# Shared-expert products added earlier in VectorE's search work, and the seam to the routed experts reordered, in a two-layer gated cross-attention kernel

## The reference

```python
x = x + tanh(g_xattn[0]) * xattn0(ctx_512, layernorm(x))      # graph from top-k similarities of ctx
x = x + tanh(g_ffn[0])   * ffn0(layernorm(x))                 # mixture of experts
x = x + tanh(g_xattn[1]) * xattn1(layernorm(x), ctx, ctx)
x = x + tanh(g_ffn[1])   * ffn1(layernorm(x))                 # block-quantized weights

# xattn0, per sequence: sim is 512 x 512
threshold = top_k(sim, 153)[..., -1]
A = sigmoid(sim) * (sim >= threshold);  A = (A + A.T) / 2
return (1 - gamma) * layernorm_x + gamma * A

# ffn0: 8 experts of 352 columns, 2 per token, and a shared one of 704 columns
y      = sum over the token's two experts of weight * (silu(x @ w1) * (x @ w3)) @ w2
shared = (silu(x @ sw1) * (x @ sw3)) @ sw2
return y + shared
```

## Time and profile before

| what | value |
|---|---|
| median of 3 runs | 1660.83 us (1656.81 to 1661.04) |
| the profiled execution | 1661.27 us |
| its span, first to last instruction | 1659.4 us |
| busy: PE, DVE, ACT, POOL | 1467.9, 1207.6, 745.5, 554.1 us |
| chain that ended last, by engine | PE 62%, DVE 20%, issue 6%, POOL 5%, ACT 3%, DMA 2% |

### The profile page before, as it was taken

How to read it: one execution, slowest core, us unless ns; L and a number is a source line. 1 busy time by engine, 2 the same in 40 slices (tenths; PEclk the granted TensorE clock), 3 DMA queues, 4 the chain that set the end, 5 groups by cost and what they waited for, 6 DMA issues and landing times.

```text
span 1659.4 us, 24186 instructions
## 1 busy us (share of the span) xinstructions
PE 1467.9 (88%) x8146; PEld 709.0 (43%) x8146; DVE 1207.6 (73%) x2087; ACT 745.5 (45%) x1346; POOL 554.1 (33%) x530
## 2 busy tenths in 40 slices
PE   3278888886999998399999999988999999999998
PEld 1144454544555554123333333324444444444444
DVE  6987777665999895899898888856556555655565
ACT  3564545223555555167777777761221222122212
POOL 2523323112776674882001000012233323332332
PEclk8589898997999999589999999999999999999999
DMA  4312222124565553663202012353000000000000
GB/s 156 105 52 66 66 66 66 46 69 146 173 199 176 182 181 129 168 149 60 56 2 48 17 18 40 52 93 61 1 0 25 0 0 0 25 0 0 25 13 13
DMA packets 114811, 113.79 MB, mean 69 GB/s; under 512 B 59416, under 2 KB 87320, under 8 KB 114720
## 3 DMA queue, kind: packets, MB, share of 16 engines
q1 hardware_dynamic: 106448, 89.64, 20.1%
q0 software_dynamic: 5680, 18.62, 4.0%
q10 hardware_dynamic: 2592, 4.39, 0.7%
HBM read 59.26 MB, written 31.20 MB: 55 GB/s over the span
## 4 chain that ended last, share of the span: by engine, by line
PE 62%; DVE 20%; issue 6%; POOL 5%; ACT 3%; DMA 2%; SPq 1%; DVEq 0%; POOLq 0%; ACTq 0%
PE PS L2215 18%; PE PS L2238 10%; PE PS L1039 9%; PE PS L1654 6%; PE PS L1643 6%; PE PS L1631 5%; PE PS L1054 4%; DVE WORK L1800 3%; PE PS L2228 2%; POOL WORK L2056 2%; POOL WORK L2063 1%; DVE WORK L695 1%; DVE WORK L722 1%; ACT BIG L1549 1%; DVE WORK L762 1%
## 5 line engine op out<-in xcount | busy, mean ns | idle before, releaser
L2215 PE MATMUL PS<-BIG 128*128 128x512 f16 x1536 | 339.9, 382 | 3.5 <-issue 2.1
L1800 DVE TENSOR_REDUCE WORK<-PS 128x2 f32<-128x1024 f32 x256 | 302.7, 1218 | 39.9 <-PE PS L1631 38.8
L1549 ACT ACTIVATE BIG<-PS 128x512 f32<-128x512 f32 x512 | 278.7, 596 | 91.3 <-PE PS L1643 86.1
L2215 PEld LDWEIGHTS PS<-BIG 128*128 128x128 f16 x1536 | 151.0, 98 | 183.7 <-issue 6.4
L1631 PE MATMUL PS<-BIG 128*128 128x512 f16 x512 | 189.3, 397 | 14.7 <-DVE WORK L1800 7.3
L1643 PE MATMUL PS<-BIG 128*128 128x512 f16 x512 | 193.3, 384 | 2.9 <-ACT BIG L1549 1.9
L1039 PE MATMUL PS<-BIG,WORK 128*128 (+1 forms) x1128 | 178.0, 315 | 16.1 <-DVE WORK L1074 9.6
L2238 PE MATMUL PS<-BIG 128*128 128x512 f16 x768 | 173.8, 379 | 1.8 <-DVE BIG L2310 1.8
L2141 ACT ACTIVATE WORK<-PS 128x512 f32<-128x512 f32 x64 | 38.1, 597 | 298.8 <-PE PS L2215 298.8
L2290 DVE SCALAR_TENSOR_TENSOR BIG<-PS,WORK 128x512 f32<-128x512 f32 x64 | 44.2, 690 | 138.8 <-ACT WORK L2141 138.7
L1039 PEld LDWEIGHTS PS<-BIG,WORK 128*128 128x128 f16 x1128 | 108.6, 98 | 79.0 <-issue 22.6
(11 more groups left out here) (257 smaller groups left out, 2228.5 us busy)
## 6 DMA issues: line engine op xcount, KB each, us to landing
wdq_scratch<-WORK SPq DMA_DIRECT2D x48, 256.0 KB, 2.2
WORK<-in_L_ffn_w_dram SPq DMA_DIRECT2D x32, 352.0 KB, 3.5
y_scratch<-WORK SPq DMA_DIRECT2D x39, 256.0 KB, 2.0
BIG<-BIG SPq DMA_DIRECT2D x96, 64.0 KB, 2.3
X<-in_x_dram SPq DMA_DIRECT2D x4, 1024.0 KB, 9.1
WORK<-in_L_ffn_w_dram SPq DMA_DIRECT2D x16, 256.0 KB, 2.6
WORK<-in_L_ffn_gate_w_dram SPq DMA_DIRECT2D x16, 256.0 KB, 3.2
WORK<-in_L_ffn_up_w_dram SPq DMA_DIRECT2D x16, 256.0 KB, 3.2
```

The source lines that it names most:

```text
L1549: nc.scalar.activation(PB[:, tp, 2 * h + j, :], src, ACT.Exp, scale=SOFT_SCALE).then_inc(exp_ok, 1)
L1800: v.tensor_reduce(MXU[:, g % 2, c:c + 2], APAIR[h % 2], AX_X, ALU.max, negate=True).then_inc(max_ok, 1)
L2215: ins = nc.tensor.matmul(bank[b], fxT[:, p, a, k * P:(k + 1) * P], w[:, c, l, k, :], start=(i == 0), stop=(i == 3 * KD - 1))
```

## The change

In the first stage `y_in` leaves the start of `half(u)` for the first three cycles and is written into the work between the half tiles: the product of the cycle before's last tile inside `search_step(a, 2)` behind its two counting passes; those of the cycle's tiles behind the third of four `window`s, behind `check_threshold`, and behind the second `norm` at the cycle's end. In the last cycle it stays at the start of `half(u)`, but for i = 0.

At the seam, ScalarE's splits of expert 6's first three chunks move from in front of the silu of the last half tile to behind it, and all of expert 7's splits move into the slots (three chunks in slot 0, two each in slots 1 and 2). VectorE does both `rows_hot` before the splits of chunks 1 and 2, and copies the indices (L1265) before it makes the expert table; chunks 3 to 6 of expert 6 are split behind that. In a slot, `fast_lo` moves in front of `w_first`.

```diff
@@ a_scalar, last cycle
-                if i == 7:
-                    act.wait_ge(SH.hg_mm, 2 * TT - 1)
-                    fast_hi(act, 8, E - 2, range(NBUF))
                 act_sil(act, SH, HOME, h, u, pair_of(f, i))
                 act_thi(act, SH, near((u - 1) // 2), 1 - h, u - 1)
...
-            fast_hi(act, 8, E - 2, (NBUF,))
+            fast_hi(act, 8, E - 2, range(NBUF))
             act_thi(act, SH, HOME, 1, 2 * TT - 1)
-            fast_hi(act, 8, E - 2, range(NBUF + 1, NCH))
-            fast_hi(act, 9, E - 1, range(NBUF))
+            fast_hi(act, 8, E - 2, range(NBUF, NCH))
@@ a_vector
-            def search_step(b, n):
+            def search_step(b, n, t=None):
...
+                if t is not None:
+                    y_in(t)
@@ half(u)
-                if h == 0 and t >= 2:
+                if f == B - 1 and h == 0 and i > 0:
                     y_in(t - 2)
@@ cycles
-                search_step(a, 2)
+                search_step(a, 2, t1 - R - 1 if f else None)
                 window((0,))
                 half(u + 2)
                 window((1,))
                 half(u + 3)
-                window((2, 3))
+                window((2,))
+                y_in(t1 - R)
+                window((3,))
                 half(u + 4)
                 pick_threshold()
                 half(u + 5)
                 check_threshold(a)
+                y_in(t1 - R + 1)
                 adjacency(a)
...
                 norm(t1 + 1)
+                y_in(t1 - R + 2)
                 if c < B:
                     search_start(c)
@@ end of the first stage
-            rows_hot(0)
             low(2 * TT - 1)
-            fast_lo(dve, 8, E - 2, range(1, NBUF))
+            rows_hot(0)
             rows_hot(1)
             v.nop().then_inc(hot_ok, 1)
-            fast_lo(dve, 8, E - 2, (NBUF,))
+            fast_lo(dve, 8, E - 2, range(1, NBUF))
             y_in(TT - 1)
-            fast_lo(dve, 8, E - 2, range(NBUF + 1, NCH - 1))
@@ b_scalar, slot
-                if first:
-                    fast_hi(act, 9, E - 1, LAST_CHUNKS[p])
+                if i < len(LAST_CHUNKS):
+                    fast_hi(act, 9, E - 1, LAST_CHUNKS[i])
...
-        LAST_CHUNKS = (range(NBUF, NCH - 2), range(NCH - 2, NCH))
+        LAST_CHUNKS = ((0, 1, 2), (3, 4), (5, 6))
@@ b_vector
+            dve.wait_ge(map_mm, 1)
+            v.tensor_copy(IDX, bank[2][:, 0:SLOTS]).then_inc(idx_ok, 1)
             v.tensor_copy(POS, POSF).then_inc(pos_ok, 1)
...
-            dve.wait_ge(eid_ok, 1)
-            dve.wait_ge(map_mm, 1)
-            v.tensor_copy(IDX, bank[2][:, 0:SLOTS]).then_inc(idx_ok, 1)
-            fast_lo(dve, 8, E - 2, (NCH - 1,))
-            fast_lo(dve, 9, E - 1, range(NBUF))
+            fast_lo(dve, 8, E - 2, range(NBUF, NCH))
             dve_lo(dve, MO, HOME, 0, 0)
@@ b_vector, slot
                 if not last:
                     dve_lo(dve, MO, HOME, 1 - p, i + 1)
+                if i < len(LAST_CHUNKS):
+                    fast_lo(dve, 9, E - 1, LAST_CHUNKS[i])
                 for n in units(i)[0:1]:
                     w_first(dve, link, n)
...
-                if first:
-                    fast_lo(dve, 9, E - 1, LAST_CHUNKS[p])
```

More of the change, by code:

```diff
@@ L926, in a_vector @@
                 dve.wait_ge(xn_st[p], 8 * TT)
+            low(2 * TT - 1)
             rows_hot(0)
-            low(2 * TT - 1)
-            fast_lo(dve, 8, E - 2, range(1, NBUF))
             rows_hot(1)
             v.nop().then_inc(hot_ok, 1)
-            fast_lo(dve, 8, E - 2, (NBUF,))
+            fast_lo(dve, 8, E - 2, range(1, NBUF))
             y_in(TT - 1)
-            fast_lo(dve, 8, E - 2, range(NBUF + 1, NCH - 1))
         class Rows:
```

## The result

The changed kernel takes 1644.03 us (median of 4 runs, 1643.27 to 1649.63) against 1660.93 for the kernel before: a ratio of 0.9909, 95% interval 0.9886 to 0.9933. That is faster, inside the predicted range of 1632 to 1652, and 4 us short of the predicted gain. The profiled execution took 1643.61 us (span 1641.7); busy are PE 1463.1, DVE 1208.8, ACT 745.2 and POOL 555.6 us, all within 5 us of before.

A forecast was written before the change was run, and what follows sets the result against it. It took TensorE and VectorE, neither full, to wait for each other in turn, with TensorE losing 24.9 us to `y_in`. Cycles 17.4, seam 7.1 and slots -3.3 sum to 21.2 off 1661.27: 1640 us, range 1632 to 1652.

The forecast's parts named there:

- The third rival: Cycles: several waits of 0.5 to 3 us could keep the granted clock at 0.50; 24 us slower, 1685; chance 0.04.
- Cycles 2 and 3: VectorE's idle time goes and the fourth window moves behind `y_in`: 6.9 and 6.6 us gained.
- VectorE does set the pace up to step 4: Cycles: the gain follows VectorE's lost idle time and moved windows, not the sum of TensorE's waits of 1.95 and 4.35.
- 3.8 + 0.7: Cycle 1: 3.76 us for the window moved behind `y_in`, plus half of 1.4 us saved on slow matmuls.
- the first rival: Cycles: hidden half tiles become what TensorE waits for, only moved windows count; cycles 10, total 1651 us; chance 0.20.
- The seam: From the last half tile to the routed stage: indices copied 7.1 us earlier, bounds 4 and 8.
- The second condition: Seam: expert 6's last chunk, read only after chunk 3's split, is ready at 378.7 us, against 379.3.
- the fixed distance from transpose to matmuls: Seam: fetch and TensorE's transpose follow the earlier index copy at their distance, so 7.1 us counts as gained.
- So I count no loss: Seam: VectorE's `rows_hot` takes 2.29 us beside GpSimd's multiplication and 2.28 without, so running them together costs nothing.
- The slots: Slot 2: `w_first(0)` waits for a weight read issued behind expert 7's last splits; 3.3 us lost, bounds 2 and 6.
- The sum: Whole kernel: 17.4 for cycles plus 7.1 for the seam less 3.3 for the slots, 21.2 us gained.
- 1.95 and 3.56: Cycles: behind a 1.95 us wait the clock stays at 1.00; behind 3.56 the nine matmuls are slow, 3.51 to 4.00.

The follow-up runs named there:

- run 1: The kernel before with only the moves of `y_in` in the four cycles, seam and slots as before: 1644.6 us, ratio 0.9901.
- run 5: Changed kernel with the `y_in` that stood behind the third window put in front of that window: 1642.76 us, ratio 0.9887.
- run 10: The kernel of run 9 with GpSimd's additions also ahead of its two splits of step 5, in all cycles: 1637.38 us, ratio 0.9855.
- run 12: The kernel of run 9 with GpSimd's additions ahead of its splits of step 5 in cycle 1 alone: 1631.55 us, ratio 0.982.
- run 9: Changed kernel plus GpSimd's additions held behind adjacency, expert 7's last chunks in slot 1, `y_in` one window sooner, first table and third split sooner: 1632.3 us.
- run 2: Changed kernel with the `y_in` in front of adjacency put behind it: 1644.17 us, ratio 0.9897.
- run 11: Changed kernel with expert 7's first three chunks split in the seam again, the other four in slots 0 and 1: 1645.81 us, ratio 0.9901.
- run 3: Changed kernel with GpSimd's four additions of own similarities held until adjacency is done: 1637.92 us, ratio 0.9861.
- run 8: Changed kernel with GpSimd's multiplication of `tile_hot` held until both `rows_hot` are done: 1644.92 us, one time only.
- run 4: Changed kernel with expert 7's last two chunks split in slot 1, not slot 2, so the read for `w_first(0)` is issued sooner: 1643.76 us, ratio 0.9898.

## Why the prediction came out as it did

- **The direction and the mechanism were right.** TensorE stood still for `y_in` with the product ready, and earlier `y_in` took 18.8 of the 24.9 us away; run 1 shows that the moves alone give the whole gain. The third rival, a clock low throughout, did not come: the mean granted clock over the whole span is 0.949 against 0.947.
- **Cycles 2 and 3 came near their terms**: 8.2 and 6.4 us by the medians (6.3 and 6.3 in this pair), predicted 6.9 and 6.6. VectorE does set the pace up to step 4, and a wait near 3 is left at step 4 of cycle 2 (3.54), as the text said; in cycle 3 it is 0.91. By run 5 the 3.54 is one window that `y_in` need not stand behind.
- **The step that failed is cycle 1**, "3.8 + 0.7" less 0.6: 3.9 us predicted, 1.6 in this pair and nothing by the median. Up to step 6 the gain is 5.5, over the 4.5. It is then given back. TensorE comes to the transposes of adjacency 5.5 us sooner than before, but adjacency starts only 3.4 us sooner, meets GpSimd's splits and additions and takes 6.88 us where it takes 2.73 with GpSimd idle; so TensorE waits 3.57 us where it did not wait at all. Steps 6 and 7 take 22.3 to 25.0 us in the seven kernels with these cycles, 18.46 before, and 18.46 again in runs 10 and 12, which keep GpSimd away (beside the edits of run 9). In five of the seven the clock fell as well behind this wait, which made up to 2.5 us of it (last section). The prediction counted what stands in front of adjacency (`y_in`, to which run 2 gives 1.2 us of the wait in cycle 1) and not what runs beside it. In part the first rival was right: in this cycle VectorE became what TensorE waits for.
- **The seam was sized at 7.1 and gave 4.8.** The chain to the index copy came 4.4 us sooner: the last half tile's matmuls took 5.42 us and not 3.74 (1.7; the granted clock was 0.70, and 1.00 before), and the two `rows_hot` lost 0.97 to GpSimd; 7.1 - 1.7 - 1.0 = 4.4. The second condition, chunk 6, was named, with a margin of 0.6 us to the fetch; it ended last. What the text did not see is that the fixed distance from transpose to matmuls holds only because expert 7's splits leave the seam (run 11).
- **"So I count no loss" was a misreading.** In the earlier trace rows the `rows_hot` kept 2.29 us beside GpSimd because there GpSimd was the one shut out: its multiplication took 4.51, and 2.54 in the changed kernel, where VectorE pays instead: the multiplication ran on for 1.07 us behind the start of the two `rows_hot` (351.20 + 2.54 - 352.67), and they lost 0.97. The rule that I set aside is that of the Trainium skill, "SBUF — State Buffer", section "Who interferes with whom": an exclusive lock between the two engines. The traces agree with it: the four instructions of adjacency take 6.88, 4.86 and 2.73 us in the changed kernel and in runs 3 and 10, by how much GpSimd does beside them, and in run 8 both sides lose once more.
- **The slots came out right, in part by luck**: +3.3 predicted in slot 2 and 3.3 there. The read was counted at 3.5 us and cost 2.55; TensorE's wait was counted at 3.1 and is 1.95. The rest is the lower clock behind this wait, which the sum had at nothing. 0.8 more came in slots 0 and 1 and behind.
- **The sum** was 21.2; of this pair's 17.7 in span, 14.9 are in these stretches, and 2.7 are in a stretch that did not change and can't be told from scatter. What stays open is the exact loss in cycle 1: before has one trace here, and its own scatter is not known.

## What to carry to other kernels

When a wait of one engine is taken away, follow the work that moves forward to its new neighbours: an instruction that comes earlier can meet another engine's work that it used to miss. To judge whether two engines disturb each other, compare the durations of both, beside each other and apart; the one that keeps its time may only be the one that came first. And where several steps must be done before the next stage, work out the time of each of them, for the second one takes over as soon as the first is moved.

## What the runs showed of the hardware

The same wait does not always bring the same clock. In cycle 1, behind a wait of 3.57 us for adjacency, the granted clock stayed at 1.00 in the changed kernel and was 0.69 over the same work in run 4; this is why steps 6 and 7 took 22.4 us in one and 24.9 in the other. The stretches, first of the changed kernel (the second line is cycle 2, behind the wait of 3.54), then of run 4 (columns as in the earlier trace rows):

```profile
141.70:147.50 5.80, 5.77 (x33) 3.67 (x33) 4.81 (x11) 0.73 (x2) 2.25 (x2) 1.00 0.00 1
...
192.40:196.20 3.80, 3.77 (x9) 1.31 (x10) 3.63 (x8) 0.86 (x2) 2.48 (x2) 0.50 0.00 0
```

```profile
142.00:150.30 8.30, 8.21 (x32) 4.87 (x33) 5.00 (x11) 0.67 (x2) 2.31 (x2) 0.69 0.00 0
```

And a wait of 2.18 left the nine matmuls at 2.11 us in the changed kernel, one of 2.16 in run 5 was followed by 3.78:

```profile
183.56 0.55 PE L1046 MATMUL PS<-ident,BIG 128*128 128x128 f32 x3 [2.16 <-DVE BIG L1077]
183.94 3.78 PE L1053 MATMUL PS<-BIG 128*128 128x512 f16 x9
```

The last half tile's matmuls follow a wait of 2.24 or 2.25 us in the first stage's last step: they took 3.74 before and in run 3, and 5.42 in the changed kernel. A price by the length of a wait alone, as the prediction had it for 1.95 and 3.56, is not to be had from these traces.
